# Forward transform of a two-layer convolution kernel: image blocks as stationary operand of TensorE, a 68-column cosine/sine table streaming

## The chip, the cores and the metric

The kernel runs on one core of a Trainium2 chip. The metric is the device time in microseconds (us) of one execution; the time of a kernel is the median over its runs. Everything is in 32-bit floats. Engines are named as the profile names them: PE is TensorE's matrix multiply, PEld its weight load (the load of the stationary operand), DVE is VectorE, ACT ScalarE, POOL GpSimd, SP SyncE, which here only issues transfers.

## The reference, cut to what matters

The input x has the shape (8, 64, 256, 256): batch, channels, height, width. Layer 0 is a gated channel mix and gives a new x of the same shape. Layer 1 is the spectral convolution, and the change lies in its first step:

```python
x_ft = jnp.fft.rfft2(x)                                   # x here: the normed output of layer 0
top = jnp.einsum('bixy,ioxy->boxy', x_ft[:, :, :m1, :m2], w1)     # m1 = m2 = 32
bot = jnp.einsum('bixy,ioxy->boxy', x_ft[:, :, -m1:, :m2], w2)
...
return jnp.fft.irfft2(out_ft, s=(h, w))
```

Only 64 of the 256 row frequencies (0 to 31 and -32 to -1) and 32 column frequencies are needed of the forward transform. A real image gives a negative row frequency from the cosine and the sine sum of the positive one, so 33 cosine and 33 sine sums over the height do.

## The kernel before, in words

The program runs stage after stage with a barrier between them: statistics of x, small preparations, layer 0's mix (it writes its result to a scratch tensor in HBM, x1_scratch), a small stage for the second norm, the **forward stage**, the mixing of the modes, the inverse stage. The change touches only the forward stage, lines 799 to 1077.

The forward stage goes through the 8 batches in four passes of a loop, two batches each (j is 0 or 1; the first pass stands unrolled ahead of the loop). A batch is read in 8 groups of 8 channels. A group's tile `x_tile` is 128 x 2 x 8 x 256: partition p holds row p in half 0 and row 128 + p in half 1. SP loads it with two transfers of 1 MB (line 845), four tiles deep (`KEPT`), and the last four stay in SBUF for the inverse stage.

Each batch has three steps on the data:

1. DVE adds the two halves of a tile (line 1006, `fwd_sum`), POOL subtracts them (line 1076, `fwd_diff`). Even row frequencies need only the sum, odd ones only the difference.
2. The rows. For every two channels (a unit; 32 units, `NR`, in a batch), PE multiplies two 128 x 64 tables (stationary) with 512 columns of the sum and of the difference (line 868), side by side in the two column halves of the array. ACT copies the 128 x 512 result from PSUM to SBUF (line 982, `fwd_rows`), PE transposes it in four 128 x 128 blocks (line 879), and DVE copies the transposed blocks, reordered, into `fwd_cols` (A in the code; line 1051, two copies a unit and two instructions a copy in the trace's count).
3. The columns, one batch later. 17 pairs of row frequencies, four matmuls each (line 900), with 128 x 128 blocks of A stationary and a 128-column table streaming; in five parts, put in between the units of the next batch (`part_after`). ACT and DVE copy the parts out of PSUM (lines 964 and 1022), DVE finishes the batch (line 1030) and ACT stores it with three transfers (line 972).

The order on PE is written out by hand: the rows of unit n + 1, then the transposes of unit n, then perhaps a part of the columns. A 32-bit matmul is two instructions in the trace, each with a weight load of its own: 68 column matmuls a batch are 136 rows of PE and 136 of PEld. The transposes are one instruction each. At the end the columns of the last batch stand alone.

Of the kernel before, what the change touches and what calls it, by code (L numbers as in the profile page):

```python
# [47 lines left out]
NP = (NM + 1) // 2  # L48
KX = 2 * M1
# [7 lines left out]
def constants():  # L57
# [56 lines left out]
def program(nc, x, w1m, b1m, w2m, b2m, sa1, sa2, gamma, beta, wr1, wi1, wr2, wi2, const, out):  # L114
    top = ExitStack()
    with top:
# [684 lines left out]
        with ph:  # L801
            T = table(ph, ["ident", "frow", "fcol"])
            ident = T["ident"][0]
# [3 lines left out]
            ED = [[sb(ph, f"fwd_{n}{i}", [P, CG, W]) for n in ("sum", "diff")] for i in range(2)]  # L807
            RS = [sb(ph, f"fwd_rows{i}", [P, 512]) for i in range(2)]
# [4 lines left out]
            sum_done, diff_done = sem("fwd_sum"), sem("fwd_diff")  # L813
            row_done, row_out, tr_done, tr_out = (sem("fwd_" + n) for n in ("row", "row_out", "tr", "tr_out"))
            col_done, col_act, col_dve = (sem("fwd_" + n) for n in ("col", "col_act", "col_dve"))
            cur, neg_done, modes_stored = (sem("fwd_" + n) for n in ("cur", "neg", "stored"))
            NR = C // 2
# [5 lines left out]
            def part_after(n):  # L823

                g = n % NR
                return g // 4 + 1 if g % 4 == 3 and g // 4 + 1 < PARTS else None

            def copy_after(n):

                g = n % NR  # L830
                return g // 4 if g % 4 == 2 and g // 4 < PARTS else None

            with nc.Block() as block:
                @block.sync
                def _(sp):
                    for n in ("ident", "frow", "fcol"):
# [16 lines left out]
                def _(pe):  # L853
                    pe.sem_inc(row_done, 8)
                    pe.sem_inc(tr_done, 2)
                    pe.wait_ge(tab, 48)

                    def rows(i, n):


                        G0, cp = n // 4, n % 4
                        if cp == 0:
                            pe.wait_ge(sum_done, i * (2 * NG) + G0 + NX + 1)
                            pe.wait_ge(diff_done, i * (2 * NG) + G0 + NX + 1)

                        pe.wait_ge(row_out, i * (2 * NR) + n + 1)
                        for par in range(2):
                            last = nc.tensor.matmul(bank(n % 2, 512, C, par * C), frow[:, par, :],  # L868
                                                    ED[G0 % 2][par][:, 2 * cp:2 * cp + 2, :],
                                                    start=True, stop=True)  # L870
                        last.then_inc(row_done, 1)

                    def transposes(i, n):
                        pe.wait_ge(row_out, i * (2 * NR) + 2 + n + 1)

                        pe.wait_ge(tr_out, i * (2 * NR) + n + 1)
                        for q in range(4):
                            at = (2 + n % 2) * 512 + q * P
                            last = nc.tensor.transpose(psum[:, at:at + P], RS[n % 2][:, q * P:(q + 1) * P], ident)  # L879
                        last.then_inc(tr_done, 1)  # L880

                    def columns(c, buf, m, first=False):

                        if m == 0:

                            pe.wait_ge(tr_out, c * NR + NR + 2)
# [19 lines left out]
                    def body(i, first):  # L906
                        for j in range(2):
                            c, skip = i * 2 + j - 1, first and j == 0
                            one = first and j == 1
                            if j == 1:  # L910
                                rows(i, NR)
                            if not skip:
                                columns(c, 1 - j, 0, one)
                            if j == 0:
                                rows(i, 0)
                            for n in range(j * NR, (j + 1) * NR):
                                m = None if skip else part_after(n)
                                if n + 1 < (j + 1) * NR:
                                    rows(i, n + 1)
                                transposes(i, n)  # L920
                                if m is not None:
                                    columns(c, 1 - j, m, one)
# [28 lines left out]
                def _(act):  # L951
                    act.sem_inc(row_out, 2)

# [21 lines left out]
                    def body(i, first):  # L975
                        for j in range(2):
                            c, skip = i * 2 + j - 1, first and j == 0
                            for n in range(j * NR, (j + 1) * NR):
                                act.wait_ge(row_done, i * (2 * NR) + 8 + n + 1)

                                act.wait_ge(tr_done, i * (2 * NR) + n + 1)
                                nc.scalar.activation(RS[n % 2][:, :], bank(n % 2), ACT.Copy).then_inc(row_out, 1)  # L982
                                if not skip:
                                    if copy_after(n) in ON_ACT:
                                        copies(c, copy_after(n), first)
                                    if n % NR == 4 * PARTS + 2:
                                        store(c, bass.ds(c, 1))
# [10 lines left out]
                def _(dve):  # L998
                    dve.sem_inc(tr_out, 2)
                    dve.sem_inc(sum_done, NX)  # L1000

                    def sums_of(i, G0):
                        dve.wait_ge(loaded[G0 % NX], loaded_by(i, G0))

                        dve.wait_ge(row_done, i * (2 * NR) + 4 * G0 + 4)
                        nc.vector.tensor_tensor(ED[G0 % 2][0][:, :, :], XW[G0 % NX][:, 0, :, :],
                                                XW[G0 % NX][:, 1, :, :], ALU.add).then_inc(sum_done, 1)
# [25 lines left out]
                    def body(i, first):  # L1033
                        sums_of(i, 0)
                        for j in range(2):
# [6 lines left out]
                            for n in range(j * NR, (j + 1) * NR):  # L1042
                                if n % 4 == 1 and n // 4 + 1 < 2 * NG:
                                    sums_of(i, n // 4 + 1)
                                c0 = n % NR * 2
                                dve.wait_ge(tr_done, i * (2 * NR) + 2 + n + 1)
                                src = bank(2 + n % 2).rearrange("p (c a m) -> p c a m", c=2, a=2)
                                dst = A[j][:, :, :, c0:c0 + 2].rearrange("p a m c -> p c a m")
# [5 lines left out]
                                if not skip:  # L1054
                                    if copy_after(n) in ON_DVE:
                                        copies(c, copy_after(n), first)
                                    if n % NR == 4 * PARTS:
# [9 lines left out]

                @block.gpsimd
                def _(pool):
                    pool.sem_inc(diff_done, NX)  # L1070
                    with pool.Fori(0, B // 2) as i:
                        for G0 in range(2 * NG):
                            pool.wait_ge(loaded[G0 % NX], loaded_by(i, G0))

                            pool.wait_ge(row_done, i * (2 * NR) + 4 * G0 + 4)
                            nc.gpsimd.tensor_tensor(ED[G0 % 2][1][:, :, :], XW[G0 % NX][:, 0, :, :],  # L1076
                                                    XW[G0 % NX][:, 1, :, :], ALU.subtract).then_inc(diff_done, 1)
# [274 lines left out]
```

## Time and profile before

| | before |
|---|---|
| median of 3 runs | 3146.73 us (3139.76 to 3147.95) |
| the profiled execution: its time | 3143.03 us |
| its span in the profile | 3141.4 us |
| forward stage, first tile landed to last column matmul | 1485.2 to 2076.1 us of the span |
| mean granted TensorE clock, whole span | 0.924 of full speed |

The full speed of TensorE is 2.4 GHz; the other level seen is half of it, 1.2 GHz. A clock of 0.95 for a stretch means that it ran at half speed for a tenth of it.

### The profile page before, as it was taken

How to read it: one execution, taken by the hardware profiler on the slowest of the kernel's cores; microseconds unless marked ns; L12 is line 12 of the kernel's file. 1: busy time of each engine (PE TensorE's matmuls, PEld its weight loads, DVE VectorE, ACT ScalarE, POOL GpSimd, SP SyncE). 2: the span in 40 equal slices, each digit the busy share in tenths (PEclk: the TensorE clock that was granted, in tenths of full speed). 3: DMA queues.
4: the chain of work that ended last, by engine and by line, in shares of the span. 5: the costliest groups of instructions: out<-in, count | busy, mean ns of one | idle time of the engine just before them, and what ended most of it. 6: DMA issues, size and time to landing. Idle time of an engine off the chain costs nothing. (4 is left out here: it accounts for less than half of the span.)

```text
span 3141.4 us, 38560 instructions
## 1 busy us (share of the span) xinstructions
PE 2248.2 (72%) x12960; PEld 1077.8 (34%) x12960; DVE 2023.4 (64%) x2317; ACT 1299.6 (41%) x1470; POOL 752.3 (24%) x477
## 2 busy tenths in 40 slices
PE   0000288888888888885999999945554898988874
PEld 0000123222323322221445444435553444444442
DVE  8999599989989998996665565620000454544442
ACT  1111188878888887885332232310000222212220
POOL 1000032332223232323655454500000111111111
PEclk9999899999999999998999999977787999998997
DMA  9999299999999999997877676569998999999999
GB/s 401 428 429 428 64 256 275 268 251 270 263 269 255 276 275 253 266 273 233 323 253 266 241 258 251 215 156 296 306 304 232 382 400 382 393 379 407 399 379 347
DMA packets 537810, 942.89 MB, mean 300 GB/s; under 512 B 16896, under 2 KB 459952, under 8 KB 493136
## 3 DMA queue, kind: packets, MB, share of 16 engines
q1 hardware_dynamic: 299264, 613.33, 62.3%
q10 hardware_dynamic: 202880, 192.95, 20.2%
q0 software_dynamic: 35536, 134.84, 11.2%
q8 instruction: 85, 1.39, 0.2%
q14 instruction: 45, 0.37, 0.0%
HBM read 647.46 MB, written 293.60 MB: 300 GB/s over the span
## 5 line engine op out<-in xcount | busy, mean ns | idle before, releaser
L617 PE MATMUL psum<-mix_x,wcur 128*64 128x512 f32 x4096 | 936.5, 613 | 154.5 <-POOL mix_x L589 135.9
L617 PEld LDWEIGHTS psum<-mix_x,wcur 128*64 128x64 f32 x4096 | 314.5, 139 | 775.9 <-issue 569.9
L1258 PE MATMUL psum<-tab_irow_icol_sign,inv_t 128*128 128x512 f32 x1024 | 495.6, 608 | 17.5 <-DVE inv_x L1305 15.4
L589 POOL TENSOR_TENSOR mix_x<-mix_x,one 64x17 f32<-64x17 f32 x256 | 318.7, 1245 | 755.1 <-DVE mix_x L691 747.6
L640 ACT ACTIVATE centred<-mix_x,pcur 64x2048 f32<-64x2048 f32 x192 | 384.5, 2003 | 206.9 <-POOL mix_x L589 190.9
L1076 POOL TENSOR_TENSOR fwd_diff<-x_tile 128x2048 f32<-128x2048 f32 x64 | 308.0, 4814 | 288.7 <-PE psum L868 255.6
L982 ACT ACTIVATE fwd_rows<-psum 128x512 f32<-128x512 f32 x256 | 152.3, 598 | 408.1 <-PE psum L868 384.1
L730 DVE SCALAR_TENSOR_TENSOR mix_out<-gated,centred 128x2048 f32<-128x2048 f32 x128 | 293.6, 2294 | 40.6 <-issue 37.3
L721 DVE SCALAR_TENSOR_TENSOR gated<-psum,pcur,gated 128x2048 f32<-128x2048 f32 x128 | 300.9, 2351 | 21.9 <-PE psum L617 20.2
L264 DVE BATCH_NORM_STATS2 stats<-stat_x 128x6 f32<-128x512 f32 x512 | 305.4, 684 | 13.6 <-DMA stat_x<-x 13.2
L1051 DVE COPY fwd_cols<-psum 128x136 f32<-128x136 f32 x512 | 154.4, 394 | 231.9 <-PE psum L879 230.9
L868 PE MATMUL psum<-fwd_sum,tab_ident_frow_fcol 128*64 128x512 f32 x512 | 281.2, 633 | 28.0 <-POOL fwd_diff L1076 18.2
L1286 ACT ACTIVATE inv_t<-psum 128x256 f32<-128x256 f32 x256 | 98.4, 385 | 477.6 <-PE psum L1249 477.6
L1121 PE MATMUL psum<-mode_w,mode_x 128*16 128x64 f32 x4096 | 170.0, 361 | 162.6 <-DMA mode_x<-modes_in 159.8
L868 PE MATMUL psum<-fwd_diff,tab_ident_frow_fcol 128*64 128x512 f32 x512 | 281.6, 634 | 0.0
L648 ACT ACTIVATE gated<-centred,pcur 128x2048 f32<-128x2048 f32 x128 | 268.4, 2097 | 11.2 <-DVE centred L699 2.9
L1305 DVE TENSOR_TENSOR inv_x<-inv_x,psum 128x1024 f32<-128x1024 f32 x128 | 155.7, 1221 | 175.6 <-PE psum L1258 142.3
L1305 DVE TENSOR_TENSOR x_tile<-x_tile,psum 128x1024 f32<-128x1024 f32 x128 | 156.2, 1221 | 166.9 <-PE psum L1258 159.1
L1258 PEld LDWEIGHTS psum<-tab_irow_icol_sign,inv_t 128*128 128x128 f32 x1024 | 199.6, 196 | 166.4 <-issue 147.1
L666 ACT ACTIVATE square<-mix_out 128x2048 f32<-128x2048 f32 x128 | 242.6, 1895 | 3.6 <-DVE mix_out L730 3.6
L296 PE MATMUL psum<-s_ones_dmask_spread_npix,w1d 128*64 128x128 f32 x1 | 0.4, 392 | 333.9 <-PEq L200 333.9
L1249 PE MATMUL psum<-tab_irow_icol_sign,inv_yy 128*128 128x256 f32 x512 | 159.7, 396 | 102.2 <-ACT inv_yy L1280 102.2
(183 smaller groups left out, 1948.6 us busy)
## 6 DMA issues: line engine op xcount, KB each, us to landing
x_tile<-x_scratch SPq DMA_DIRECT2D x184, 1024.0 KB, 7.7
mix_x<-x SPq DMA_DIRECT2D x240, 576.0 KB, 8.2
stat_x<-x SPq DMA_DIRECT2D x64, 2048.0 KB, 13.2
x_scratch<-mix_out ACTq DMA_DIRECT2D x128, 1024.0 KB, 9.0
inv_x<-x_scratch SPq DMA_DIRECT2D x64, 1024.0 KB, 11.6
out<-x_tile POOLq DMA_DIRECT2D x64, 1024.0 KB, 17.6
out<-inv_x POOLq DMA_DIRECT2D x64, 1024.0 KB, 15.6
mode_w<-L_conv_w_imag ACTq DMA_DIRECT2D x16, 2048.0 KB, 21.2
```

Source lines behind the costliest of these rows:

```text
L264: last = nc.vector.bn_stats(stats[:, at:at + 6], XT[t % NX][:, q * 512:(q + 1) * 512])
L589: last = nc.gpsimd.tensor_tensor(XT[n % NX][h, :, to], XT[n % NX][h, :, of], one[h, :], ALU.mult)
L617: last = nc.tensor.matmul(bank(k * 4 + q, 512, C, par * C), wcur[j][:, m * C:(m + 1) * C], XT[n % NX][:, r0:r0 + 3:2, m:m + W], start=(m = ...
L640: last = nc.scalar.activation(XC[n % NX][h, :].rearrange("p (r w) -> p r w", w=W), XT[n % NX][h, 1:MR:2, 1 - half:1 - half + W], ACT.Ident ...
L648: nc.scalar.activation(G[n % NX][:, :], XC[n % NX][:, :], ACT.Sigmoid, bias=pcur[j][:, 1:2], scale=pcur[j][:, 0:1]).then_inc(sig_done, 1)
L666: nc.scalar.activation(SQ[:, :], XO[k][:, :], ACT.Square, accum_out=sqs[:, bass.ds(i * NI + n, 1)]).then_inc(sq_done, 1)
L721: nc.vector.scalar_tensor_tensor(out=G[n % NX][:, :], in0=psum[:, k * SC:(k + 1) * SC], scalar=pcur[j][:, 3:4], in1=G[n % NX][:, :], op0=A ...
L730: nc.vector.scalar_tensor_tensor(out=XO[k][:, :], in0=G[n % NX][:, :], scalar=1.0, in1=XC[n % NX][:, :], op0=ALU.add, op1=ALU.mult, accum_ ...
L868: last = nc.tensor.matmul(bank(n % 2, 512, C, par * C), frow[:, par, :], ED[G0 % 2][par][:, 2 * cp:2 * cp + 2, :], start=True, stop=True)
L1076: nc.gpsimd.tensor_tensor(ED[G0 % 2][1][:, :, :], XW[G0 % NX][:, 0, :, :], XW[G0 % NX][:, 1, :, :], ALU.subtract).then_inc(diff_done, 1)
L1258: last = nc.tensor.matmul(bank(n % 2 * 2 + a), TS[n % 2][:, a * P:(a + 1) * P], icol, start=True, stop=True)
L1305: nc.vector.tensor_tensor(xw, xw, psum[:, n % 2 * 1024:n % 2 * 1024 + 1024] .rearrange("p (a k) -> p a k", a=2), ALU.add).then_inc(added, 1)
```

## The change

The sums and differences, the ACT copy and the transposes go, and POOL has nothing left in this stage. The image itself becomes the stationary operand: for each channel, each half of the columns (s) and each half of the rows (a), the 128 x 128 block of the tile is loaded as weights, and a table of 68 columns (33 cosines, 33 sines and two columns of zeros, one set for each half of the rows) streams over it. The two halves of the rows add up in PSUM. The result already has the image's columns on the partitions. A unit is now 4 channels (`RC`) and 16 matmuls; a batch has 16 units. DVE copies one unit with one instruction of 128 x 544 elements, to the same places of A. The column step is unchanged; its parts stand after units 0, 1, 3, 5 and 7 of the next batch, and ACT only copies and stores modes. A tile is free when the matmuls of its second unit are done, instead of when the sum and the difference are.

The table and SP's loads of a tile:

```diff
-    frow = np.zeros((P, 2, C))
-    for par in range(2):
-        k = np.arange(par, NM, 2)
-        a = th * np.outer(np.arange(P), k)
-        frow[:, par, :len(k)] = np.cos(a)
-        frow[:, par, NP:NP + len(k)] = np.sin(a)
+    frow = np.zeros((P, 2, 2 * NM2))
+    for half in range(2):
+        a = th * np.outer(np.arange(P) + half * P, np.arange(NM))
+        frow[:, half, :NM] = np.cos(a)
+        frow[:, half, NM2:NM2 + NM] = np.sin(a)
...
-                            sp.wait_ge(sum_done, i * (2 * NG) + G0 + 1)
-                            sp.wait_ge(diff_done, i * (2 * NG) + G0 + 1)
-                            for a in range(2):
+                            sp.wait_ge(row_done, i * (2 * NR) + 2 * G0 + 2)
+                            for a in (1, 0):
```

(`NM` is 33, `NM2` is 34.) PE, where `rows` changes, `transposes` goes and the order of the parts is new:

```diff
-                        if cp == 0:
-                            pe.wait_ge(sum_done, i * (2 * NG) + G0 + NX + 1)
-                            pe.wait_ge(diff_done, i * (2 * NG) + G0 + NX + 1)
+                        G0, c0 = n // 2, n % 2 * RC
+                        if c0 == 0:
+                            pe.wait_ge(loaded[G0 % NX], loaded_by(i, G0))
 
                         pe.wait_ge(row_out, i * (2 * NR) + n + 1)
-                        for par in range(2):
-                            last = nc.tensor.matmul(bank(n % 2, 512, C, par * C), frow[:, par, :],
-                                                    ED[G0 % 2][par][:, 2 * cp:2 * cp + 2, :],
-                                                    start=True, stop=True)
+                        for c in range(RC):
+                            for s in range(2):
+                                at = n % 2 * 1024 + c * 256 + s * 2 * NM2
+                                for a in range(2):
+                                    last = nc.tensor.matmul(psum[:, at:at + 2 * NM2],
+                                                            XW[G0 % NX][:, a, c0 + c, s * P:(s + 1) * P],
+                                                            frow[:, a, :], start=(a == 0), stop=(a == 1))
                         last.then_inc(row_done, 1)
 
-                    def transposes(i, n):
-                        pe.wait_ge(row_out, i * (2 * NR) + 2 + n + 1)
-
-                        pe.wait_ge(tr_out, i * (2 * NR) + n + 1)
-                        for q in range(4):
-                            at = (2 + n % 2) * 512 + q * P
-                            last = nc.tensor.transpose(psum[:, at:at + P], RS[n % 2][:, q * P:(q + 1) * P], ident)
-                        last.then_inc(tr_done, 1)
...
+                                rows(i, n)
+                                if not skip and n % NR == 0:
+                                    columns(c, 1 - j, 0, one)
+                                if not skip and n % 2 == 1 and n % NR // 2 + 1 < PARTS:
+                                    columns(c, 1 - j, n % NR // 2 + 1, one)
```

ACT's copy, DVE's copies (its sums, `sums_of`, go as well) and the whole program of POOL:

```diff
-                                nc.scalar.activation(RS[n % 2][:, :], bank(n % 2), ACT.Copy).then_inc(row_out, 1)
...
-                                for par in range(2):
-
-                                    last = nc.vector.tensor_copy(dst[:, :, :, par::2],
-                                                                 src[:, :, :, par * C:par * C + 2 * NP])
-                                last.then_inc(tr_out, 1)
...
+                                dve.wait_ge(row_done, i * (2 * NR) + 2 * NX + n + 1)
+                                nc.vector.tensor_copy(
+                                    A[j][:, :, :, c0:c0 + RC].rearrange("p a m c -> p c (a m)"),
+                                    psum[:, n % 2 * 1024:n % 2 * 1024 + 1024]
+                                    .rearrange("p (c m) -> p c m", c=RC)[:, :, 0:4 * NM2]).then_inc(row_out, 1)
...
-                @block.gpsimd
-                def _(pool):
-                    pool.sem_inc(diff_done, NX)
...
-                            nc.gpsimd.tensor_tensor(ED[G0 % 2][1][:, :, :], XW[G0 % NX][:, 0, :, :],
-                                                    XW[G0 % NX][:, 1, :, :], ALU.subtract).then_inc(diff_done, 1)
```

## Rows read from the trace of the kernel before

**Rows 1.** Page: the chain of work that ended last, by engine.
```profile
DMA 17%; PE 3%; issue 2%; ACT 0%; SPq 0%; POOLq 0%; POOL 0%; DVE 0%; DVEq 0%; ACTq 0%
```
**Rows 2.** Windows: PE, PEld, DVE, ACT, POOL busy (count); clock, DMA share, GB/s.
```profile
1485.20:2076.10 590.90, 547.75 (x3136) 287.70 (x3136) 345.45 (x668) 178.35 (x320) 308.03 (x64) 0.96 0.68 249
1638.00:1642.00 4.00, 4.00 (x35) 3.70 (x34) 2.23 (x7) 0.60 (x1) 3.40 (x1) 1.00 0.97 360
1471.00:1474.00 3.00, 2.40 (x18) 2.07 (x18) 0.05 (x1) 0.00 (x0) 0.00 (x0) 0.50 0.01 4
1485.00:1492.00 7.00, 0.00 (x0) 0.00 (x0) 2.29 (x1) 0.00 (x0) 6.67 (x2) 0.50 1.01 426
2121.00:2128.00 7.00, 6.33 (x161) 6.04 (x157) 0.00 (x0) 0.00 (x0) 0.00 (x0) 1.00 1.16 293
```
**Rows 3.** Groups, 1450 to 2110 us: busy us, mean ns | idle before, releaser.
```profile
L1076 POOL TENSOR_TENSOR fwd_diff<-x_tile 128x2048 f32<-128x2048 f32 x64 | 308.0, 4814 | 288.7 <-PE psum L868 255.6 <-DMA x_tile<-x_scratch 33.1
L1051 DVE COPY fwd_cols<-psum 128x136 f32<-128x136 f32 x512 | 154.4, 394 | 231.9 <-PE psum L879 230.9
L900 PE MATMUL psum<-tab_ident_frow_fcol,fwd_cols 128*128 128x128 f32 x1024 | 122.9, 280 | 8.2 <-issue 6.6 <-DVE fwd_cols L1051 1.6
L1022 DVE TENSOR_SCALAR fwd_modes<-psum,ncur 64x256 f32<-64x256 f32 x64 | 27.7, 473 | 13.1 <-PE psum L900 12.9
```
**Rows 4.** Timeline, start of the stage: start us, length us, engine [idle before].
```profile
1485.19 2.29 DVE L1006 TENSOR_TENSOR fwd_sum<-x_tile 128x2048 f32<-128x2048 f32 x1 [9.40 <-DMA x_tile<-x_scratch]
1492.09 1.09 PE L868 MATMUL psum<-fwd_sum,tab_ident_frow_fcol 128*64 128x512 f32 x1 [18.17 <-POOL fwd_diff L1076]
1496.46 0.64 PE L868 MATMUL psum<-fwd_sum,tab_ident_frow_fcol 128*64 128x512 f32 x1
```
**Rows 5.** Timeline: a steady unit from first matmul to first, and the end.
```profile
2050.97 0.64 PE L868 MATMUL psum<-fwd_sum,tab_ident_frow_fcol 128*64 128x512 f32 x1
2052.57 0.64 PE L868 MATMUL psum<-fwd_sum,tab_ident_frow_fcol 128*64 128x512 f32 x1
...
2060.49 15.58 PE L900 MATMUL psum<-tab_ident_frow_fcol,fwd_cols 128*128 128x128 f32 x136 [0.70 <-DVE fwd_cols L1051]
```
**Rows 6.** Timeline: one part of the columns between units.
```profile
1638.79 3.74 PE L900 MATMUL psum<-tab_ident_frow_fcol,fwd_cols 128*128 128x128 f32 x32
```
**Rows 7.** Groups, 2060.4 to 2080 us: weight loads of 128 and of 64 columns.
```profile
L900 PEld LDWEIGHTS psum<-tab_ident_frow_fcol,fwd_cols 128*128 128x128 f32 x128 | 14.4, 192 | 0.9 <-DVE fwd_cols L1051 0.9
L900 PEld LDWEIGHTS psum<-tab_ident_frow_fcol,fwd_cols 128*64 128x64 f32 x8 | 0.8, 136 | 0.1
```
**Rows 8.** Timeline: four instructions of 24 columns over 128 x 128 weights.
```profile
335.99 0.93 PEld L303 LDWEIGHTS psum<-raw,s_ones_dmask_spread_npix 128*128 128x128 f32 x4 [1.26 <-DVE sa2t L377]
335.99 1.05 PE L303 MATMUL psum<-raw,s_ones_dmask_spread_npix 128*128 128x24 f32 x4 [0.97 <-DVE sa2t L377]
```
**Rows 9.** Groups: the same four, and two at the low clock (1471 to 1474 us).
```profile
L303 PEld LDWEIGHTS psum<-raw,s_ones_dmask_spread_npix 128*128 128x128 f32 x4 | 0.9, 321 | 1.3 <-DVE sa2t L377 1.3
L303 PE MATMUL psum<-raw,s_ones_dmask_spread_npix 128*128 128x24 f32 x4 | 1.0, 392 | 1.0 <-DVE sa2t L377 1.0
L763 PEld LDWEIGHTS psum<-norm_values,tab_group_ident 128*128 128x128 f32 x2 | 0.5, 309 | 0.2 <-issue 0.2
L760 PE MATMUL psum<-tab_group_ident,params 64*1 64x64 f32 x16 | 1.9, 305 | 12.1 <-DMA tab_group_ident<-tables 12.1
```
**Rows 10.** Timeline: the two kinds of stall; the bracket is idle time before.
```profile
1670.03 5.08 ACTq L972 DMA_DIRECT2D modes_in<-fwd_modes  x3
1675.94 0.66 PE L879 MATMUL psum<-tab_ident_frow_fcol,fwd_rows 128*128 128x128 f32 x4 [2.73 <-ACT fwd_rows L982]
...
1765.77 4.44 PE L900 MATMUL psum<-tab_ident_frow_fcol,fwd_cols 128*128 128x128 f32 x23 [3.45 <-issue]
```
**Rows 11.** Page: a large read of PSUM, and the loads of a tile.
```profile
L1305 DVE TENSOR_TENSOR inv_x<-inv_x,psum 128x1024 f32<-128x1024 f32 x128 | 155.7, 1221 | 175.6 <-PE psum L1258 142.3
...
x_tile<-x_scratch SPq DMA_DIRECT2D x184, 1024.0 KB, 7.7
```

More of the change, by code:

```diff
@@ L48 @@
 NP = (NM + 1) // 2
+NM2 = 2 * NP
 KX = 2 * M1
@@ L806, in program @@
             NX, XW = KEPT, x1_kept
-            ED = [[sb(ph, f"fwd_{n}{i}", [P, CG, W]) for n in ("sum", "diff")] for i in range(2)]
-            RS = [sb(ph, f"fwd_rows{i}", [P, 512]) for i in range(2)]
             A = [sb(ph, f"fwd_cols{i}", [P, 2, 4 * NP, C]) for i in range(2)]
@@ L812, in program @@
             tab, loaded = sem("fwd_tables"), [sem(f"fwd_loaded{i}") for i in range(NX)]
-            sum_done, diff_done = sem("fwd_sum"), sem("fwd_diff")
-            row_done, row_out, tr_done, tr_out = (sem("fwd_" + n) for n in ("row", "row_out", "tr", "tr_out"))
+            row_done, row_out = sem("fwd_row"), sem("fwd_row_out")
             col_done, col_act, col_dve = (sem("fwd_" + n) for n in ("col", "col_act", "col_dve"))
             cur, neg_done, modes_stored = (sem("fwd_" + n) for n in ("cur", "neg", "stored"))
-            NR = C // 2
+            RC = 4
+            NR = C // RC
             PARTS = 5
             ON_ACT, ON_DVE = (0, 2), (1, 3, 4)
[L823 to L831, printed above, removed]
             with nc.Block() as block:
@@ L835, in _ @@
                 def _(sp):
-                    for n in ("ident", "frow", "fcol"):
+                    for n in ("frow", "fcol"):
                         sp.dma_start(*T[n]).then_inc(tab, 16)
@@ L909, in body @@
                             one = first and j == 1
[L910 to L915, printed above, removed]
-                            for n in range(j * NR, (j + 1) * NR):
[L917 to L922, printed above, removed]
+                            for n in range(j * NR, (j + 1) * NR):
+                                rows(i, n)
[3 more added lines that the diff above has]
+                                    columns(c, 1 - j, n % NR // 2 + 1, one)
                     body(0, True)
@@ L951, in _ @@
                 def _(act):
-                    act.sem_inc(row_out, 2)
                     def copies(c, m, first=False):
@@ L977, in body @@
                             c, skip = i * 2 + j - 1, first and j == 0
-                            for n in range(j * NR, (j + 1) * NR):
-                                act.wait_ge(row_done, i * (2 * NR) + 8 + n + 1)
-                                act.wait_ge(tr_done, i * (2 * NR) + n + 1)
-                                nc.scalar.activation(RS[n % 2][:, :], bank(n % 2), ACT.Copy).then_inc(row_out, 1)
[L983 to L987, printed above, removed]
+                            if skip:
+                                continue
+                            for m in ON_ACT:
+                                copies(c, m, first)
+                            store(c, bass.ds(c, 1))
                     body(0, True)
@@ L998, in _ @@
                 def _(dve):
[L999 to L1007, printed above, removed]
+                    dve.sem_inc(row_out, 2)
                     def take(c, cs):
@@ L1042, in body @@
                             for n in range(j * NR, (j + 1) * NR):
[L1043 to L1048, printed above, removed]
-                                for par in range(2):
-                                    last = nc.vector.tensor_copy(dst[:, :, :, par::2],
-                                                                 src[:, :, :, par * C:par * C + 2 * NP])
-                                last.then_inc(tr_out, 1)
[L1054 to L1057, printed above, removed]
+                                c0, m = n % NR * RC, n % NR // 2
+                                dve.wait_ge(row_done, i * (2 * NR) + 2 * NX + n + 1)
[3 more added lines that the diff above has]
+                                    .rearrange("p (c m) -> p c m", c=RC)[:, :, 0:4 * NM2]).then_inc(row_out, 1)
+                                if not skip and n % 2 == 1:
+                                    if m in ON_DVE:
+                                        copies(c, m, first)
+                                    if m == PARTS:
                                         finish(c)
@@ L1066, in _ @@
                     finish(B - 1)
-                @block.gpsimd
-                def _(pool):
-                    pool.sem_inc(diff_done, NX)
[L1071 to L1075, printed above, removed]
-                            nc.gpsimd.tensor_tensor(ED[G0 % 2][1][:, :, :], XW[G0 % NX][:, 0, :, :],
-                                                    XW[G0 % NX][:, 1, :, :], ALU.subtract).then_inc(diff_done, 1)
         ph = ExitStack()
```

12 lines of the change are left out of this document (4 added, 8 removed).

## The prediction

> **What bounds the kernel now.** I read the page first. Its chain that ended last [rows 1] names the inverse stage alone, 17% of the span on transfers, since that stage ends the program; barriers stand between the stages, so a microsecond won or lost in the forward stage goes through to the end whole, and the chain says nothing on its worth. The windows [rows 2] give the stage: 590.9 us, PE busy in 547.8 of them, DVE in 345, POOL in 308, the transfers at 249 GB/s where 426 GB/s were moved at the stage's start. So PE bounds it, not the transfers. The groups [rows 3] say the same from the other side: POOL sat idle for 255.6 us until PE was done with a tile.
>
> The timeline gives PE's own pace. A unit of two channels takes 1.59 us from its first matmul to the next one's [rows 5]; 256 of them make 407 us. A part of the columns is 32 instructions in 3.74 us [rows 6]; with 0.28 us for a single one [rows 3] that is (3.74 - 0.28) / 31 = 0.1116 us from one to the next at full clock [rows 2]. A batch has 136 and the stage 1088: 121.4 us. Together 528.4 us of bare work, while the first matmul starts at 1492.1 and the last ends at 2076.1: 584.0. So 55.6 us are stalls and slow clock. Two kinds of stall recur: ACT issues the three stores of a batch for 5.08 us while PE waits 2.7 us for ACT's row copy, and at the loop's jump PE stands 3.45 us [rows 10]. The granted clock over the stage is 0.96 [rows 2].
>
> **The change part by part.** *Gone.* DVE's sums and POOL's differences were 2.3 and 4.8 us a tile beside PE, hidden but for the first: the first tile lands at 1485.2, the first matmul waits until 1492.1 for the difference [rows 4]. That gives back 6.9 us. The row matmuls, transposes and ACT copies go: 407 us of PE.
>
> *Added: 2048 matmuls, 4096 instructions*, each with a load of 128 x 128 weights and 68 streaming columns. What does one cost? The trace has none like it, but both halves have rows.
> - The stream: at half clock 16 instructions of 64 columns with a load of a single column take (1.9 - 0.305) / 15 = 0.106 us each [rows 9, 2]; at full clock 68 columns are 0.056 us.
> - The load: 128 columns last 192 ns, 64 columns 136 ns [rows 7], so 64 columns more cost 56 ns and a whole block 0.112 us. The load is twice the stream.
> - Do they overlap? In the column step, 128 columns of load and 128 of stream (0.112 and 0.106) come every 0.1116 us: fully overlapped. And with a stream far shorter than the load: four instructions of 24 columns [rows 8] come every (1.05 - 0.392) / 3 = 0.219 us. Their loads last 321 ns, as those of the 309 ns row do at clock 0.50 [rows 9, 2], against 192 at full; so they ran at half clock (the window's clock isn't recorded there), and at full clock that is 0.110 us. Load and stream in a row would have been 0.213 + 0.040 = 0.253.
>
> So the weight load sets the pace, whatever the 68 columns save. I take 0.1116 us, from the column step, whose operands lie in the same way and which runs at the clock that this stage has: 4096 x 0.1116 = 457.1 us. The bounds: above, the last column step as a whole, (15.58 - 0.28) / 135 = 0.1133 us [rows 5], 464.1 us; below, the spacing of the four loads, (0.93 - 0.321) / 3 = 0.203 us [rows 8, 9], 0.102 at full clock, 417.8 us. That low value is weak, since the first of them had nothing ahead.
>
> The Trainium skill (TensorE: Matmul & The Clock Gate, "LDWEIGHTS (loading the stationary operand)") prices a load by its columns over 1.2 per ns, 107 ns here, and by it the row matmuls would be 437 us and the kernel 20 us faster than I say; the trace's spacing with full loads is 4 to 5% over it.
>
> *DVE*: a unit is now one copy of 544 elements. From the 1024-element read of PSUM [rows 11] it is 0.65 us, from four of today's copies of 394 ns [rows 3] 1.58 us. Two units take PE 7.14 us; DVE has 2 x 1.58 and four mode copies of 0.47 in them, 5.0 at most. Hidden; only at the end of the rows it shows, before the last columns: about 1.2 us, where 0.7 are now [rows 5].
>
> *Transfers*: a tile is held until its second unit is done. Tiles are used every 7.1 us or more, and three are in hand, 21 us, against 7.7 us to land [rows 11]; at the start they come every 2.1 MB / 426 GB/s = 4.9 us [rows 2]. Hidden. Cover gone, each late microsecond would be paid 64 times.
>
> *ACT*: nothing on PE's path waits for it but the columns' banks; its 5 us of issuing meet PE's next part only 9 units later. The stall of 2.7 us a batch goes. *The loop's jump*: PE's first work after it was waiting for copies until then; of the 3.45 us about 2.6 were the jump itself. Twice, and perhaps hidden under instructions already queued: I take half, 2.6 us.
>
> *The clock*: at the start matmuls last 1.09 us, 4 us later 0.64 [rows 4], so 2 us are lost, then as now.
>
> **The sum.** From the first tile at 1485.2: 0.1 for the start, 2.0 clock, 457.1 rows, 121.4 + 0.3 columns, 1.2 at the end of the rows, 2.6 jumps: 584.7 us, against 590.9. So 6.2 us are won: PE has 50 us more bare work (578.5 for 528.4), and some 49 us of stalls and slow clock and 6.9 us at the start go. The profiled execution took 3143.0 us (span 3141.4 and 1.6 around it), 3.7 under the median; carried over to the median, 3146.7 - 6.2 = 3140.5. A change of under 0.3%, 9.4 us, is about what a measurement of this kernel can't tell from none. I forecast no change: 0.46. This case's own range is 3131 to 3155: it takes the upper bound of 0.1133 (7 us more), both jumps in full, or a pace of 0.1093.
>
> **The rivals.**
> *The load is quicker than I say* (0.32, faster). With loads back to back the pace could lie between 0.102 and 0.110 us. For: the slow-clock row scales to 0.110 or less. Against: the column step's 0.1116 is measured at the clock in question. At 0.108 the rows are 442.4 us, the kernel 3125.8, with the jumps hidden 3123.2; at 0.106, 3117.5.
>
> *The clock falls in the rows* (0.12, slower). The array streams for 0.056 of every 0.112 us, half the time; before, the two column halves streamed for most of a unit. For: what the chip grants after such a stretch no row shows. Against: in the mode mixing PE ran 161 instructions of 64 columns over only 16 loaded ones in 7 us, at clock 1.00 [rows 2]. Price: half clock doubles 0.1116 us. It decides from 16 us at half clock on more than I have (8 us lost undoes the gain and more; 31 us of it make the kernel slower by 0.3%). In the eight units of each batch without columns, 28.6 us, it would cost 8 x 28.6 = 229 us: 3369.
>
> *Load and stream in a row* (0.03, slower). Then an instruction is 0.112 + 0.056 = 0.168 us, the rows 688 us, and the kernel 3371 us. Against it stand both overlaps above. The Trainium skill (same page, "The mechanism") says that a weight load overlaps a running matmul only when the row groups differ, and here they never do; by that rule the change would be this rival. The trace disagrees with it: 0.1116 us in the column step, with equal row groups.
>
> *A wait takes the place of the one removed* (0.07): a late tile or a late DVE copy at each of 128 units. Half a microsecond for each tile is 32 us: 3172. Nothing in the prices above leads there.
>
> That the change doesn't do what it says I give nothing: no option is in it that could be ignored.
>
> **How the numbers follow.** Same 0.46; faster 0.34 (the quick load and a little of the edge of the first case); slower 0.20 (clock, row, wait). Range 3118 to 3160: below it lies the unlikely half of the quick load, above it most of the slower cases.
>
> **What would show it.** Right: in the profile after, the row matmuls every 0.111 to 0.112 us with loads of about 192 ns, in 457 us; no sums, POOL empty; first matmul at about 1485.3; no idle time on PE over 1 us but at the jump. Wrong: a spacing of 0.107 (quick load), of 0.22 with loads of 310 ns (clock), of 0.17 with the clock full (in a row), or waits of PE on `x_tile` or `fwd_cols`.

## The result and the profile after

| | before | changed |
|---|---|---|
| median | 3146.24 us (4 runs) | 3205.5 us (4 runs) |
| ratio | | 1.0206, 95% interval 1.0179 to 1.0233 |
| span of the profiled execution | 3141.4 us | 3200.5 us |
| forward stage, first row matmul to end of the last column matmul | 584.0 us | 660.9 us |

The changed kernel is 2.1% slower, where no change was forecast, and it lies 45 us above the range. After the forward stage both spans are the same (1065.3 and 1065.0 us). Ahead of it they aren't: the last matmul of the second norm, up to which the code is the same, ended 11.7 us earlier in the changed kernel's profile (1462.2 us of the span, against 1473.9). So the stages are compared by their own length here: 76.9 us more from first to last matmul, less 5.8 us that the first one starts sooner after the norm's last (12.4 us instead of 18.2).

The windows of the changed kernel; columns as in [rows 2]. The first line is the whole stage, the next three follow one another in time, the last is a later one.

```profile
1474.60:2135.60 661.00, 647.16 (x5184) 644.72 (x5184) 175.47 (x220) 26.12 (x64) 0.00 (x0) 0.89 0.60 222
1474.60:1592.80 118.20, 118.15 (x554) 118.18 (x555) 18.37 (x18) 0.00 (x0) 0.00 (x0) 0.50 0.49 187
1592.80:1806.20 213.40, 213.40 (x1904) 212.53 (x1903) 64.45 (x81) 9.80 (x24) 0.00 (x0) 1.00 0.67 248
1806.20:1821.50 15.30, 9.32 (x43) 9.33 (x44) 2.16 (x3) 0.00 (x0) 0.00 (x0) 0.55 0.66 266
...
1962.10:1978.60 16.50, 9.92 (x47) 9.93 (x48) 2.16 (x3) 0.00 (x0) 0.00 (x0) 0.59 0.62 247
```

The reader is to see three things. PE is busy for 647.2 of 661.0 us, so idle time is 14 us of the stage and can't be most of what was lost. The first 118.2 us run at clock 0.50, with PE busy throughout, 554 instructions of 0.213 us each; in [rows 2] the granted clock of the stage was 0.96, here it is 0.89. Then the clock is 1.00 for 213 us, until a stretch of 15.3 us with 6 us of idle time and a clock of 0.55; the last line is a second such stretch, 156 us later.

The timeline of the changed kernel, lines of PE: the start of the stage, a stretch at full clock in which rows and columns follow each other, the end of the rows, and the last columns.

```profile
1474.65 25.63 PE L855 MATMUL psum<-tab_frow_fcol,x_tile 128*128 128x68 f32 x119 [12.42 <-DMA x_tile<-x_scratch]
...
1639.78 20.49 PE L855 MATMUL psum<-tab_frow_fcol,x_tile 128*128 128x68 f32 x182
...
2107.82 10.99 PE L855 MATMUL psum<-tab_frow_fcol,x_tile 128*128 128x68 f32 x97
...
2119.97 15.58 PE L878 MATMUL psum<-tab_frow_fcol,fwd_cols 128*128 128x128 f32 x136 [1.16 <-DVE fwd_cols L1000]
```

At the start 119 instructions take 25.63 us; at the end 97 take 10.99, and (10.99 - 0.28) / 96 is 0.1116 us. That is to the fourth place the pace that was forecast for full clock. The last columns start 1.16 us after the rows.

The groups of the same kernel, against [rows 3]:

```profile
L855 PE MATMUL psum<-tab_frow_fcol,x_tile 128*128 128x68 f32 x4096 | 524.6, 296 | 25.0 <-issue 12.6 <-DMA x_tile<-x_scratch 12.4
L1000 DVE COPY fwd_cols<-psum 128x544 f32<-128x544 f32 x128 | 139.7, 1091 | 482.5 <-PE psum L855 482.5
L878 PE MATMUL psum<-tab_frow_fcol,fwd_cols 128*128 128x128 f32 x1024 | 124.1, 281 | 1.2 <-DVE fwd_cols L1000 1.2
```

The row matmuls are busy 524.6 us instead of the 457.1 forecast. PE's only waits are "issue", 12.6 us in two pieces, the first tile, and the 1.2 us before the last columns. DVE waits for PE, and its copy of 544 elements is 1.09 us.

### The profile page after: what moved, and what is told of

Read it like the earlier page. It is cut to its first block and busy times, and to the rows that moved or that the text cites. A ratio compares the mean times of both kernels' runs of the same rounds, so it can differ in the third digit from the quotient of the medians.

```text
span 3200.5 us, 40715 instructions
## 1 busy us (share of the span) xinstructions
PE 2339.3 (73%) x15008; PEld 1433.2 (45%) x15008; DVE 1853.7 (58%) x1869; ACT 1146.2 (36%) x1214; POOL 459.4 (14%) x413
## 5 line engine op out<-in xcount | busy, mean ns | idle before, releaser
L855 PE MATMUL psum<-tab_frow_fcol,x_tile 128*128 128x68 f32 x4096 | 524.6, 296 | 25.0 <-issue 12.6
L855 PEld LDWEIGHTS psum<-tab_frow_fcol,x_tile 128*128 128x128 f32 x4096 | 522.2, 213 | 26.6 <-issue 26.6
L589 POOL TENSOR_TENSOR mix_x<-mix_x,one 64x17 f32<-64x17 f32 x256 | 334.1, 1305 | 726.9 <-DVE mix_x L691 719.5
L1000 DVE COPY fwd_cols<-psum 128x544 f32<-128x544 f32 x128 | 139.7, 1091 | 482.5 <-PE psum L855 482.5
L933 ACT ACTIVATE fwd_modes<-psum,ncur 64x256 f32<-64x256 f32 x64 | 26.1, 456 | 642.9 <-PE psum L878 642.7
L1256 POOL DMA_DIRECT2D out<-x_tile x64 | 56.5, 887 | 1376.3 <-DVE x_tile L1244 1126.4
L1060 PEld LDWEIGHTS psum<-mode_w,mode_x 128*16 128x16 f32 x4096 | 162.6, 140 | 170.6 <-issue 169.9
```

What stands on the lines that cost most here:

```text
L589: last = nc.gpsimd.tensor_tensor(XT[n % NX][h, :, to], XT[n % NX][h, :, of], one[h, :], ALU.mult)
L855: last = nc.tensor.matmul(psum[:, at:at + 2 * NM2], XW[G0 % NX][:, a, c0 + c, s * P:(s + 1) * P], frow[:, a, :], start=(a == 0), stop=(a = ...
L1060: last = nc.tensor.matmul(psum[32 * k:32 * k + 2 * B, at:at + C], XM[j][:, :, kx * M2 + ky], WT[j][:, :, k * M2 + ky], start=True, stop=True)
```

## The experiments

The theory after the result: the pace is right, and three things on the clock and the jump cost the 76 us. (a) The rows of 68 columns don't bring the clock back once it is at half. The first batch has no column parts between its units, so it stays at half for 118 us, until 2 us into the first column part. 554 instructions were done in that time, 61.8 us of work at 0.1116: 56.4 us lost where 2 were forecast. (b) The two jumps of PE's loop cost 6.0 and 6.6 us of idle time instead of 1.3 each. (c) The clock falls in the gap of each jump and comes back only in the next column part: 9.3 and 9.8 us of work there ran at half, some 9.2 us lost. 54.4 + 10.0 + 9.2 = 73.6, of 660.9 - 584.6 = 76.3.

The second column of times is the kernel before on the chip of the same runs. The stage's length is that from the first row matmul to the end of the last column matmul, and it is what the runs are compared by: ahead of the stage, where the code is the same in all, the norm's last matmul ended anywhere from 1469 to 1480 us of the span in twelve of the thirteen profiles, and at 1462 in the changed kernel's. The median of a single run holds such a difference whole.

| run | median, us | before on that chip | stage, us | mean clock in the stage |
|---|---|---|---|---|
| changed kernel | 3205.5 | 3146.2 | 660.9 | 0.89 |
| e1_pad128 | 3151.0 | 3146.2 | 600.9 | 0.99 |
| e2_warm (one run) | 3160.6 | 3146.2 | 603.4 | 0.98 |
| e3_unroll (one run) | 3193.5 | 3146.2 | 640.3 | 0.91 |
| e4_pad128_unroll | 3137.5 | 3146.2 | 585.6 | 1.00 |
| e5_hold_loads (one run) | 3204.5 | 3144.4 | 652.1 | 0.90 |
| e6_before_unroll | 3136.9 | 3144.4 | 576.8 | 0.98 |
| e7_pad128_unroll_warm | 3134.9 | 3144.4 | 582.8 | 1.00 |
| e8_half_load (one run) | 2951.1 | 3144.4 | 402.0 | 0.98 |
| e9_before_unroll_sp_store | 3113.8 | 3148.1 | 551.7 | 1.00 |
| e10_unroll_warm (one run) | 3131.4 | 3148.1 | 582.4 | 1.00 |
| e11_before_unroll_again | 3140.3 | 3148.1 | 581.1 | 0.97 |

**e1_pad128.** The table is widened with zeros; DVE's copy picks the same 68 columns of each half.

```diff
+FW = 128
-    frow = np.zeros((P, 2, 2 * NM2))
+    frow = np.zeros((P, 2, FW))
...
-                                at = n % 2 * 1024 + c * 256 + s * 2 * NM2
+                                at = n % 2 * 1024 + c * 256 + s * FW
...
-                                    last = nc.tensor.matmul(psum[:, at:at + 2 * NM2],
+                                    last = nc.tensor.matmul(psum[:, at:at + FW],
```

> The table is filled up with zero columns, so that 128 columns stream over each loaded block instead of 68; nothing else changes (DVE picks the same 68). Theory (the clock doesn't come back while the array streams only half the time; the pace is set by the weight load anyway): the row matmuls stay at 0.112 us at full clock, the clock is full about 4 us after the first matmul instead of 118 us, and the half-clock time after each jump of PE's loop ends about 4 us after the first matmul too. Gain about 57 + 5 us on the changed kernel: near 3143 us, no different from the kernel before. Rival (the clock is low for another reason, such as the long idle time ahead of the stage or the 128-wide loads): no gain, near 3205 us, first rows still every 0.213 us. Rival (the stream costs after all): rows slower than 0.112 us at full clock.

Measured: 3150.99 us, ratio to before 1.0014 (0.9998 to 1.0029), 54.5 us less than the changed kernel and 8 over the expected 3143; stage 600.9, 60.0 less of the 62 expected. Windows of e1: the first four microseconds, the next 67, and the stage.

```profile
1488.80:1493.00 4.20, 4.19 (x23) 4.20 (x24) 0.00 (x0) 0.00 (x0) 0.00 (x0) 0.60 1.00 421
1493.00:1560.00 67.00, 67.00 (x602) 67.00 (x602) 19.81 (x19) 1.60 (x4) 0.00 (x0) 1.00 0.82 314
1488.80:2089.70 600.90, 587.33 (x5184) 584.37 (x5184) 176.31 (x220) 26.11 (x64) 0.00 (x0) 0.99 0.66 245
```

The clock is full within about 4 us of the first matmul, with the same loads, the same tiles and nearly the same idle time ahead (10.8 us, 12.4 in the changed kernel). Behind the first jump it comes back in the rows too: the 32 instructions there took 5.76 us, 7.09 in the changed kernel. 602 instructions in 67.0 us are 0.111 us each: 60 columns more a matmul cost nothing. So both parts hold: the stream of 68 or of 128 columns doesn't set the pace, and with 128 columns the clock rises in rows in which with 68 it stayed down. The rivals fall.

**e2_warm.** Rows of 68 columns, and ahead of them, while the first tile is on its way:

```diff
+                    for _ in range(10):
+                        nc.tensor.matmul(bank(7), fcol[:, 0, 0, :], T["fcol"][0],
+                                         start=True, stop=True)
```

> Ten matmuls of 512 columns are put ahead of the first row matmul, in the time in which PE waits for the first tile; the rows keep their 68 columns. Their result is not used. Theory (rows of 68 columns can't bring the clock back but don't let it fall either): the clock is full when the first row matmul starts and stays full until the first jump of the loop, the first batch takes 57 us instead of 114; the two jumps still cost as much as before. Near 3148 us. Rival (68-column rows let the clock fall again): the first batch is slow again after some us; near 3200 us.

Measured: one time, 3160.59 us; stage 603.4, 57.5 less. The timeline of PE and the windows of e2:

```profile
1476.29 10.66 PE L843 MATMUL psum<-tab_frow_fcol 128*128 128x512 f32 x20 [5.37 <-DMA tab_frow_fcol<-tables]
1486.79 13.40 PE L858 MATMUL psum<-tab_frow_fcol,x_tile 128*128 128x68 f32 x119
```

```profile
1477.00:1486.80 9.80, 9.80 (x21) 4.12 (x20) 0.00 (x0) 0.00 (x0) 0.00 (x0) 0.85 1.01 425
1486.80:1545.00 58.20, 58.20 (x523) 58.20 (x522) 17.25 (x16) 0.00 (x0) 0.00 (x0) 1.00 0.82 318
```

The ten matmuls bring the clock up, and then the same rows that stood at 0.50 for 118 us run 58.2 us at 1.00. The time is 12 us over the expected 3148, though the stage's gain is as forecast: the first row came 15.9 us after the norm's last matmul, behind the ten, where in the changed kernel it came after 12.4, and in this execution the norm itself ended 8.7 us later than in the changed kernel's.

**e3_unroll.** PE's loop written out.

```diff
-                    body(0, True)
-                    with pe.Fori(1, B // 2) as i:
-                        body(i, False)
+                    for i in range(B // 2):
+                        body(i, i == 0)
```

> PE's loop over the batches is written out, so PE jumps nowhere in the stage. Theory: the two idle times of 6.0 and 6.6 us are gone and with them the two stretches of 13.7 us at half clock (about 10 us lost in them); the first batch stays at half clock. Gain 12.6 + 9.6 = 22 us: near 3183 us. Rival (the idle times are waits for DVE or instruction supply that comes at that place anyway): they stay, near 3205 us.

Measured: one time, 3193.52 us, 10 over the expected 3183, in an execution whose norm ended 10.8 us later than the changed kernel's; stage 640.3, 20.6 less than the changed kernel where 22 were expected. Windows of e3: the first batch, then all the rest.

```profile
1484.10:1605.00 120.90, 120.83 (x566) 120.86 (x567) 18.35 (x18) 0.00 (x0) 0.00 (x0) 0.50 0.48 187
1605.00:2124.50 519.50, 518.32 (x4620) 516.12 (x4618) 157.09 (x202) 26.12 (x64) 0.00 (x0) 1.00 0.65 239
```

No idle time but the 1.2 us before the last columns, and no slow clock after the first batch, which stays as slow as it was. (b) and (c) hold and are apart from (a).

**e4_pad128_unroll.** Both edits.

> Both: 128 streaming columns and PE's loop written out. Theory: row matmuls 4096 x 0.1117 = 457 us and columns 121.5 us with nearly no stall, forward stage about 584 us less 4 from its first matmul to its last; about 77 us less than the changed kernel, near 3130 us, 0.5% faster than the kernel before. Rival (either effect has another cause): 3143 us or more.

Measured: 3137.54 us, ratio 0.9966 (0.9944 to 0.9987). The stage as one window:

```profile
1488.80:2074.50 585.70, 584.48 (x5184) 581.90 (x5184) 176.42 (x220) 26.12 (x64) 0.00 (x0) 1.00 0.68 250
```

585.6 us from first matmul to last column. The prediction's sum gives 584.6 us for that stretch with the jumps and 582.0 without; the slow clock at the start was 0.8 us more than its 2.0, and 2.8 us are left, 0.5%. With (a), (b) and (c) taken away the rest of the sum stands. The median is 7.5 us over the expected 3130, a number that hung on the changed kernel's median, whose runs are few; 3146.2 times the interval is 3129 to 3142.

**e5_hold_loads.** The question here is why the jump of PE's loop costs more than before. In the trace the jump is a branch on the sequencer that feeds PE (PEldq). The view of one line, of the changed kernel (first fence) and of the kernel before (second); the columns are count, shortest, median and longest in ns. The shortest is the branch that is not taken at the end.

```profile
L896 PEldq COMPARE_BRANCH  x3: 83/7700/8397, 1804.1 to 2116.8; - x3
```

```profile
L925 PEldq COMPARE_BRANCH  x3: 79/3326/3538, 1761.9 to 2059.2; - x3
```

7.7 and 8.4 us where it was 3.3 and 3.5. The transfers around the branch, 1804 to 1812 us in the changed kernel and 1761 to 1766 in the kernel before:

```profile
DMA packets 410, 2.90 MB, mean 363 GB/s; under 512 B 57, under 2 KB 57, under 8 KB 57
```

```profile
DMA packets 129, 0.90 MB, mean 180 GB/s; under 512 B 20, under 2 KB 20, under 8 KB 20
```

Tiles and modes are in transfer in the first, at twice the rate of the second, where the last tile had nearly landed. The one edit:

```diff
-                            sp.wait_ge(row_done, i * (2 * NR) + 2 * G0 + 2)
+                            sp.wait_ge(row_done, i * (2 * NR) + (2 * NX + 1 if G0 == 1 else 2 * G0 + 2))
```

> The changed kernel, with one number changed in SP's waits: the second tile of each pass of the loop (and with it the third and fourth, which stand behind it) is loaded only when the first unit of that pass is done, so that no tile is in transfer when PE jumps. Theory (PE's jump, 7.7 and 8.4 us where it was 3.5 and 3.3 before, is long because its instructions are fetched behind the tile loads that now run at that moment, where before the change all tiles had landed by then): the branch takes about 3.5 us again, of which 2 are hidden, and PE is idle for 1.5 to 2 us instead of 6.0 and 6.6. Rival (the branch is long because the loop's body has more instructions): 7 us or more as before. The time as a whole may be lost in part to later tiles: 3195 to 3210 us.

Measured: one time, 3204.47 us; stage 652.1. The branch in e5, first at 1814.2 us, and the transfers of the four microseconds that it took:

```profile
L896 PEldq COMPARE_BRANCH  x3: 83/3699/3743, 1814.2 to 2117.0; - x3
```

```profile
DMA packets 49, 0.28 MB, mean 70 GB/s; under 512 B 16, under 2 KB 16, under 8 KB 16
```

70 GB/s, and these are stores of modes. Around the second branch nothing but one packet of instructions was in transfer (1969 to 1972 us), and it took as long. The same code branches in 3.7 us when no tile is on its way, and PE idles 1.94 us instead of 6.0. So it was the transfers, not the length of the body. The stage is 8.8 us shorter than the changed kernel's, as much as PE's idle time at the jumps fell (12.6 to 3.9); the time as a whole isn't, in an execution whose norm ended 8.7 us later. The traces show one packet of instructions (0.02 MB) fetched near each jump, but not what held it, so "fetched behind the tiles" is a reading, if a likely one. The clock fell after 1.94 us of idle time too: the next rows took 7.09 us for 32 instructions.

**e6_before_unroll and e11_before_unroll_again.** The kernel before with e3's edit. e11 is the same kernel once more, beside e9.

> The kernel before, with PE's loop over the batches of the forward stage written out. Theory: its two idle times of 3.45 and 3.14 us at the jump shrink to about 1 us of waiting for the last copies, and the 3.4 us of half clock behind each goes too: 2 x (2.3 + 1.7) = 8 us less than the kernel before, near 3138 us, the same as the changed kernel with 128 columns and the loop written out; then the change of the row step itself is worth nothing beyond a microsecond or two. Rival (the jump costs the kernel before nothing, since DVE is late there anyway): 3146 us.

> The kernel before with only PE's loop written out, again, for a comparison on the same chip as the version with stores on SP: near 3137 us by every theory.

Measured: 3136.94 us, ratio 0.9970 (0.9953 to 0.9986), and 3140.34, 0.9974 (0.9959 to 0.9990). The loop's jump was worth 8 us in the kernel before as well. Hence e4's gain over the kernel before is the loop's, not the change's: with both loops written out, the kernel before (0.9970) and the change with 128 columns (0.9966) stand at the same ratio.

**e7_pad128_unroll_warm.** e4 with four of e2's matmuls.

> The changed kernel with 128 streaming columns, PE's loop written out and four unused 512-column matmuls ahead of the first tile. Against the same without them, the half-clock time of the first rows (5.7 us, 2.8 lost) goes: near 3135 us, 0.3 to 0.5% faster than the kernel before. If the four matmuls hold up the first row matmul by 2 us or more, nothing is left of it.

Measured: 3134.92 us, ratio 0.9970 (0.9946 to 0.9994); stage 582.8, 2.8 less than e4, as expected; no time at half clock. It is the fastest version of the change that has several runs (e10 below has one), and on the same chip the kernel before with its loop written out is at 3136.94: no difference.

**e8_half_load.** The kernel leaves out half of the image's columns: each matmul loads 64 columns of a block.

```diff
-                                    last = nc.tensor.matmul(psum[:, at:at + 2 * NM2],
-                                                            XW[G0 % NX][:, a, c0 + c, s * P:(s + 1) * P],
+                                    last = nc.tensor.matmul(psum[0:64, at:at + 2 * NM2],
+                                                            XW[G0 % NX][:, a, c0 + c, s * P:s * P + 64],
```

> The changed kernel, but each row matmul loads only 64 of a block's 128 image columns; the sums of the other half are left out. The 68-column stream stays. Theory (the load sets the pace): with 64 loaded columns (0.056 us) and 68 streaming ones (0.057) the spacing falls from 0.112 to about 0.06 us at full clock, half in both; the array then streams nearly all the time and the clock is full about 4 us after the first matmul. PE's rows would take 250 us, and the tile loads (134 MB at 300 to 400 GB/s) or DVE's copies set the stage instead. Rival (something else, such as a fixed cost per instruction, sets 0.112): the spacing stays.

Measured: one time, 2951.12 us; stage 402.0. Its timeline:

```profile
1493.20 4.00 PE L855 MATMUL psum<-tab_frow_fcol,x_tile 128*64 128x68 f32 x64 [1.62 <-DMA x_tile<-x_scratch]
```

64 instructions in 4.00 us: (4.00 - 0.23) / 63 = 0.060 us. The time of an instruction halves with the load while the stream stays, so the load set it. The window from 1486.8 to 1490.0 us, which begins 5.0 us after the first matmul:

```profile
1486.80:1490.00 3.20, 3.20 (x57) 3.20 (x56) 1.37 (x2) 0.00 (x0) 0.00 (x0) 1.00 1.04 438
```

The clock is full, with 68 columns: the short stream alone doesn't keep it down, but a short stream beside a load twice as long does. The expectation that the tiles would then set the stage failed: PE was busy for 382 of the 402 us and waited 7.3 us for tiles after the first, at 385 GB/s from 1490 to 1850 us.

**e10_unroll_warm.** 68 columns, e3's edit and four of e2's matmuls.

> The changed kernel with its 68 columns, the loop written out and four unused 512-column matmuls ahead of the first tile. Theory (68 columns hold a full clock once it is full, and nothing else is wrong with them): no time at half clock in the stage, length from first row matmul to last column 583 us as with 128 columns, near 3135 us. Rival (the clock falls in some unit without columns, 28 us a batch): more time at half clock.

Measured: one time, 3131.37 us; stage 582.4, no time at half clock. The 68 columns hold a full clock through every stretch without column parts, the whole first batch included. Padding is one way out, a start at full clock without a gap another.

**e9_before_unroll_sp_store.** If stalls were what the change removed, they can be removed where they are. The kernel before, e3's edit, and the stores moved from ACT to SP, ahead of the load of the second tile of the next batch but one. The main part of the edit; the issuing itself, SP's unrolled first pass and PE's written-out loop aren't shown:

```diff
+                            if not first and G0 % NG == 1:
+                                c = i * 2 + G0 // NG - 2
+                                sp_store(c, bass.ds(c, 1))
 
                             sp.wait_ge(sum_done, i * (2 * NG) + G0 + 1)
...
-                                    if n % NR == 4 * PARTS + 2:
-                                        store(c, bass.ds(c, 1))
```

> The kernel before with PE's loop written out and the three stores of a batch issued by SP instead of ACT, so that ACT never stands 5 us with a row copy behind it. Theory (stalls are what the change removed, and they can be removed without the 50 us of extra weight loads): the seven idle times of 1.5 to 3.0 us behind ACT (15 us) go, with most of the 25 us at half clock that follow them (12 us lost): about 27 us less than with the loop alone, near 3112 us, 1% faster than the kernel before and faster than every version of the change. Rival (PE then waits for DVE's late sum at the same places, since DVE finishes the batch there): only a few us, near 3133 us.

Measured: 3113.76 us, ratio 0.9896 (0.9879 to 0.9913), against 3140.34 for the loop alone on the same chip: 26.6 us less, 27 expected. Of PE's waits in the stage, the one behind ACT in the kernel before, and two that are left in e9 (columns: us in total, times, longest; L879 and L894 are the transposes, L883 the rows):

```profile
PE psum L879 <- ACT fwd_rows L982: 15.5, 7, 3.0
```

```profile
PE psum L883 <- DVE fwd_sum L1017: 8.8, 8, 1.2
PE psum L894 <- DVE fwd_cols L1062: 2.8, 4, 0.7
```

No wait for ACT is left on PE, the clock no longer falls after the start (1.00 over the stage), and PE still waits up to 1.2 us a batch for DVE's sum, as it did before (9.4 us in all). This kernel beats the kernel before by 34 us on the same chip, and by its median the changed kernel by 92.

## Why the prediction was wrong

- **The pace of the row matmuls** ("I take 0.1116 us ... 457.1 us"): right. 0.1116 at full clock; e1 and e8 show from both sides that the load sets it. The rival "load and stream in a row" wanted 0.168 and is refuted, and so is the quick load.
- **The start** (6.9 us given back): 5.8 by the distance from the norm's last matmul.
- **The columns** (121.7) **and the end of the rows** (1.2): 1.16 us at the end and 15.58 us for a batch of columns. Right.
- **DVE** (0.65 to 1.58 a copy, hidden): 1.09 and hidden. (The trace has two copies a unit in the kernel before, of one instruction each, 512 for 256 units, and not two instructions a copy.) **Transfers** hidden: PE waited for no tile but the first. Right.
- **The stalls behind ACT** go: right, no such wait is left.
- **The clock** ("4 us later 0.64, so 2 us are lost, then as now"): this step failed. I took the 4 us from rows in which 512 columns streamed and gave them to rows that stream 68 beside a load twice as long. It was 118 us, 56.4 lost. The rival of the falling clock looked at the right thing, a stream half as long as its load, and its sign came (0.22 with loads of 310 ns was named; 0.213 with loads of 333 ns was measured in the first batch). But it feared that a full clock would fall in the units without columns, and e10 shows that it holds; what doesn't happen is that a half clock rises. It counted eight such units a batch and left out that the first batch has no columns in any of its sixteen. Its price of 229 us was for a case that isn't there, and the range left both out.
- **The loop's jump** ("I take half, 2.6 us"): 12.6 us. The jump's cost in the kernel before was read rightly (in e6, without it, PE's idle time ahead of the columns is 2.8 us where it was 8.2, so 2.7 a jump). The hiding was right too: 2.1 us of each branch lie under queued matmuls. But the branch itself took 7.7 and 8.4 us in place of 3.3 and 3.5, because tile loads now run at that moment (e5). I had costed the later release of the tiles by their arrival alone and not by what else they meet. And behind each jump the clock came back late again, 9.2 us, the same failed step once more.

The terms that held give 580.0 us from the first row on, without jumps and slow clock, and e10, which has neither, measured 582.4. Those 2.4 us are in the changed kernel too; with the failed terms, 54.4 + 10.0 + 9.2, they make up the 76 us.

What stays open: by the profiles the change costs 71 us at the end of the stage (76.9 - 5.8), by the medians 59. The profiles differ by 59 as well at the end of the program, since the norm ended 11.7 us sooner in the changed kernel's, the earliest of the thirteen. Whether that belongs to this one execution or to the kernel isn't known: the medians of four runs speak for the kernel, e3 and e5, whose code up to there is the same (1473 and 1471 us), for the execution. No run here was made for it. That tile loads lengthen the branch rests on one run (e5). What in the rows keeps the clock from rising isn't settled beyond this: with a longer stream (e1) and with a shorter load (e8) it rises.

## What to carry to other kernels

Cost a new matmul by the larger of load and stream, and then ask separately whether its mix of the two will bring a half clock back: rows of another shape don't answer that, and the stages with nothing else between such matmuls are where it shows. A loop's jump on the bounding engine costs more when transfers run beside it, and it can pull the clock down behind it; writing the loop out is a cheap test. Before replacing work to be rid of stalls, price the stalls by themselves: here 50 us of extra work bought less than a written-out loop and three transfers issued by another engine did without any.

## What the runs showed of the hardware

- One kernel, the same row matmuls (68 columns over 128 x 128 loads, PE busy all the time): 116 us at 1.2 GHz when they began there, 58 us and more at 2.4 GHz when they began there (e2), and 582 us with the column parts between (e10). At 1.2 GHz the clock rose 2 us into the first column part.
- 128 streamed columns instead of 68 over the same load cost nothing: 0.111 us an instruction, at both widths.
- The branch back of PE's loop: 3.3 to 3.7 us with no tile or the end of one in transfer (70 and 180 GB/s), 7.7 and 8.4 us with tiles in transfer (363 GB/s).
- A gap of 1.94 us on PE was followed by 32 rows at half clock (e5).
- Three stores issued by ACT held it for 5.1 us [rows 10]; issued by SP (e9), no wait of PE for ACT or for a tile is left in the stage.
